# A routing stage with its sums on VectorE from SBUF, transposes in four PSUM banks and ranks behind the second gate

## What is computed

```python
x = x + _L0_gnn_ref(_layernorm(x, axis=-1), src, dst, edge_weight)   # 25000 edges, sums in float16
# feed-forward: h = layernorm(x)
logits = h @ gate_w + gate_b                    # 50000 x 8
idx = argmax(softmax(logits)); prb = its probability
pos = (cumsum(one_hot(idx)) * one_hot(idx)).sum(-1) - 1     # the token's rank with its expert
kept = pos < C                                  # C = ceil(1.25 * 50000 / 8)
y = (relu(buf @ w1 + b1) @ w2 + b2)[idx, pos] * (prb * kept)
x = x + y
```

## Time and profile before

| | before |
|---|---|
| median of three runs | 3391.64 us |
| profiled execution | 3385.78 us |
| its span | 3384.2 us |
| PE busy | 2856.8 us (84%) |
| DVE busy | 2205.4 us (65%) |
| ACT busy | 1627.8 us (48%) |
| POOL busy | 1881.3 us (56%) |
| mean granted clock of PE | 0.886 |

### The profile page before, as it was taken

One profiled execution on the slowest core, in us unless ns is written; L12 is line 12 of the kernel. 1 busy time (PEld: TensorE's weight loads), 2 busy tenths in 40 slices (PEclk: granted clock), 3 DMA queues, 4 the chain that ended last, 5 costly groups with the idle time before them and its releaser, 6 DMA issues.

```text
span 3384.2 us, 63776 instructions
## 1 busy us (share of the span) xinstructions
PE 2856.8 (84%) x20366; PEld 2577.6 (76%) x20367; DVE 2205.4 (65%) x5550; ACT 1627.8 (48%) x2915; POOL 1881.3 (56%) x1680
## 2 busy tenths in 40 slices
PE   5733323289899976999999999999999999999998
PEld 4733223278788866989889898989899889898987
DVE  7934343377766644677766767777767676767766
ACT  3412121156655644555554555555555555555554
POOL 7788888756766765436354334536343454335333
PEclk8766666678867868999999999999999999999999
DMA  9644443386766623112112111212111121111111
GB/s 375 193 77 71 69 88 58 52 321 230 245 207 221 234 75 101 45 39 74 39 50 69 44 45 45 67 36 71 45 50 44 42 69 48 44 43 47 41 46 45
DMA packets 182245, 322.06 MB, mean 95 GB/s; under 512 B 97649, under 2 KB 124348, under 8 KB 166256
## 3 DMA queue, kind: packets, MB, share of 16 engines
q0 software_dynamic: 89696, 146.98, 16.7%
q1 hardware_dynamic: 92288, 172.66, 15.0%
q10 hardware_dynamic: 144, 1.05, 0.1%
HBM read 186.52 MB, written 138.79 MB: 96 GB/s over the span
## 4 chain that ended last, share of the span: by engine, by line
PE 57%; DVE 3%; issue 1%; DVEq 0%; POOL 0%; DMA 0%; SPq 0%; ACT 0%; POOLq 0%
PE u_Y L1353 29%; PE u_H L1339 26%; PE u_T L1321 2%; DVE y L1283 1%; DVE y L1278 1%; DVE yo L1297 1%; DVE yo L1294 0%; DVE low L1288 0%; DVE yo L1292 0%; DVE hlo L1265 0%; POOL u_x L1141 0%; DVEq L1264 0%; DMA u_x<-out_x,u_rec 0%; DVE u_token L1291 0%; DMA u_rec<-slots 0%
## 5 line engine op out<-in xcount | busy, mean ns | idle before, releaser
L1166 POOL DMA_INDIRECT out_x<-yo,u_token x348 | 435.8, 1252 | 761.0 <-DVE yo L1299 664.2
L1353 PE MATMUL u_Y<-whi,hhi 128*128 128x256 f32 x2784 | 788.2, 283 | 22.2 <-DVE hlo L1265 22.2
L1216 ACT ACTIVATE hm<-u_H,b1e 128x512 f32<-128x512 f32 (+1 forms) x736 | 489.0, 664 | 644.5 <-PE u_H L1339 618.9
L1353 PE MATMUL u_Y<-wlo,hhi 128*128 128x256 f32 x2784 | 779.7, 280 | 0.0
L1353 PE MATMUL u_Y<-whi,hlo 128*128 128x256 f32 x2784 | 779.4, 280 | 0.0
L1141 POOL DMA_INDIRECT u_x<-out_x,u_rec x380 | 396.5, 1043 | 363.4 <-issue 330.0
L1339 PE MATMUL u_H<-xhi,whi 128*128 128x512 f32 (+1 forms) x1472 | 571.5, 388 | 10.1 <-issue 10.1
L1339 PE MATMUL u_H<-xlo,whi 128*128 128x512 f32 (+1 forms) x1472 | 564.8, 384 | 0.0
L1339 PE MATMUL u_H<-xhi,wlo 128*128 128x512 f32 (+1 forms) x1472 | 564.5, 384 | 0.0
L1353 PEld LDWEIGHTS u_Y<-whi,hhi 128*128 128x128 f32 x2784 | 526.1, 189 | 25.3 <-DVE hlo L1265 25.3
L1353 PEld LDWEIGHTS u_Y<-wlo,hhi 128*128 128x128 f32 x2784 | 526.1, 189 | 0.0
(11 more groups left out here) (154 smaller groups left out, 4710.5 us busy)
## 6 DMA issues: line engine op xcount, KB each, us to landing
x<-in_x SPq DMA_DIRECT2D x49, 1024.0 KB
out_x<-x SPq DMA_DIRECT2D x49, 1024.0 KB, 5.0
agg<-zeros SPq DMA_DIRECT2D x25, 1024.0 KB
at<-agg SPq DMA_DIRECT2D x49, 512.0 KB, 5.8
raw<-in_L_ffn_w POOLq DMA_DIRECT2D x14, 1024.0 KB
src_row<-in_src SPq DMA_DIRECT2D x25, 512.0 KB, 4.8
slots<-rec,slot_i POOLq DMA_INDIRECT x392
u_x<-out_x,u_rec POOLq DMA_INDIRECT x380
```

What stands on the lines that cost most here:

```text
L1166: pool.indirect_dma_start(out=out[:, :], out_offset=bass.IndirectOffsetOnAxis(ap=token[:, s:s + 1], axis=0), in_=yo[:, s, :], in_offset=No ...
L1216: act.activation(hm[:, f, cols], ps_H[:, f % 2, cols], ACT.Relu, bias=b1e[:, f:f + 1])\
L1353: last = pe.matmul(ps_Y[:, s, 0:D], a[:, f, rows], w2_at(w, buf, f), start=(f == 0 and j == 0), stop=(f == KF - 1 and j == 2))
```

## The change

`add` reads `at` from SBUF instead of its copy in PSUM, and waits for the load itself. `aggregate`, `ident16`, `ps_A` and `agg_up` are gone; SP's `load` waits for `x1_ready` four steps back. The four PSUM banks go to `ps_T`, one for each quarter, `ps_L` gets two banks, one for every other step, and the unread products get a bank of their own. `gated` is raised by every gate, and a copy waits for the same quarter's gate of the step before. `fill` issues three products of 512 columns in place of four of 384. The order of a step on PE becomes turn 0, turn 1, turn 2, fill, gate 0, turn 3, gate 1, rank of the step before, gate 2, fill, gate 3.

```diff
-    ident16 = sb("ident16", [P, P], F16)
...
-    ps_A = ctx.enter_context(nc.psum_tensor("ps_A", [P, G, D], F32))
-    ps_T = ctx.enter_context(nc.psum_tensor("ps_T", [P, 2, 4, P], F32))
-    ps_L = ctx.enter_context(nc.psum_tensor("ps_L", [P, 512], F32))
+    ps_T = ctx.enter_context(nc.psum_tensor("ps_T", [P, 4, 4, P], F32))
+    ps_L = ctx.enter_context(nc.psum_tensor("ps_L", [P, 2, 512], F32))
     ps_R = ctx.enter_context(nc.psum_tensor("ps_R", [P, 512], F32))
-    logits = ps_L[:, 0:G * E].rearrange("p (g e) -> p g e", g=G)
+    unread = ctx.enter_context(nc.psum_tensor("unread", [P, 4, P], F32))
+    logits = ps_L[:, :, 0:G * E].rearrange("p b (g e) -> p b g e", g=G)
     ranks = ps_R[:, 0:(G + 1) * E].rearrange("p (g e) -> p g e", g=G + 1)
-    unread = ps_L[:, P:4 * P].rearrange("p (n c) -> p n c", n=3)
-    FILL = 4
+    FILL = 3
...
                 if not (isinstance(i, int) and s < AGGS):
-                    sp.wait_ge(agg_up, s + 1 - AGGS)
+                    sp.wait_ge(x1_ready, s + 1 - AGGS)
                     sp.nop(nofuse=True)
...
-                    if k == 0 and not (isinstance(i, int) and s < 1):
-                        act.wait_ge(gated, s)
+                    if not (isinstance(i, int) and s < 1):
+                        act.wait_ge(gated, BANKS * (s - 1) + k + 1)
                     act.wait_ge(turned, BANKS * s + k + 1)
                     part = slice(k * PER_BANK, (k + 1) * PER_BANK)
-                    act.activation(hT[:, part, :], ps_T[:, k % 2], ACT.Copy).then_inc(hT_ready, 1)
+                    act.activation(hT[:, part, :], ps_T[:, k], ACT.Copy).then_inc(hT_ready, 1)
...
+                normalise(2)
                 copy(0)
-                normalise(2)
+                normalise(3)
                 copy(1)
-                normalise(3)
                 copy(2)
                 copy(3)
...
-            def aggregate(i, r):
-                s = RING * i + r
-                pe.wait_ge(agg_loaded[r % AGGS], 16 * ((RING // AGGS) * i + r // AGGS + 1))
-
-                if not (isinstance(i, int) and s == 0):
-                    pe.wait_ge(x1_ready, s)
-                for g in range(G):
-                    last = pe.matmul(ps_A[:, g, :], ident16[:], at[:, r % AGGS, g, :], start=True, stop=True)
-                last.then_inc(agg_up, 1)
...
                 if k == 0:
-                    if not (isinstance(i, int) and s < 1):
-                        pe.wait_ge(hot_ready, s)
-                    pe.matmul(logits, ident[:], gb[:].unsqueeze(1).broadcast_to([P, G, E]),
+                    if not (isinstance(i, int) and s < 2):
+                        pe.wait_ge(hot_ready, s - 1)
+                    pe.matmul(logits[:, q], ident[:], gb[:].unsqueeze(1).broadcast_to([P, G, E]),
...
-                if k == BANKS - 1:
-                    last.then_inc(gated, 1)
+                last.then_inc(gated, 1)
...
                 for _ in range(FILL):
-                    pe.matmul(unread, ones[:], before[:].unsqueeze(1).broadcast_to([P, 3, P]),
-                              start=False, stop=True, skip_group_check=True)
+                    pe.matmul(unread[:], ones[:], before[:].unsqueeze(1).broadcast_to([P, 4, P]),
+                              start=True, stop=True)
...
-                if not (isinstance(i, int) and s < 1 and k < 2):
-                    pe.wait_ge(hT_ready, BANKS * s + k - 1)
+                if not (isinstance(i, int) and s < 1):
+                    pe.wait_ge(hT_ready, BANKS * (s - 1) + k + 1)
...
                 turn(i, r, 0)
                 turn(i, r, 1)
-                if isinstance(i, int) and s == 0:
-                    aggregate(0, 2)
-                else:
+                turn(i, r, 2)
+                fill()
+                gate(i, r, 0)
+                turn(i, r, 3)
+                gate(i, r, 1)
+                if not (isinstance(i, int) and s == 0):
                     rank(*before_of(i, r, 1))
-                    fill()
-                gate(i, r, 0)
-                turn(i, r, 2)
-                gate(i, r, 1)
-                turn(i, r, 3)
-                if not (isinstance(i, int) and s == 0):
-                    fill()
                 gate(i, r, 2)
-                if not (isinstance(i, int) and s > LAST - 3):
-                    aggregate(*((i, r + 3) if r + 3 < RING else (i + 1, r + 3 - RING)))
+                fill()
                 gate(i, r, 3)
...
-                v.wait_ge(agg_up, s + 1)
+                v.wait_ge(agg_loaded[r % AGGS], 16 * ((RING // AGGS) * i + r // AGGS + 1))
                 v.wait_ge(x_loaded[r], 16 * (i + 1))
-                v.tensor_tensor(x1[:, r], ps_A[:], x1[:, r], ALU.add).then_inc(x1_ready, 1)
+                v.tensor_tensor(x1[:, r], at[:, r % AGGS], x1[:, r], ALU.add).then_inc(x1_ready, 1)
...
-                v.wait_ge(gated, s + 1)
-                v.tensor_reduce(top[:], logits, AX.X, ALU.max).then_inc(chosen, n.inc())
+                v.wait_ge(gated, BANKS * (s + 1))
+                v.tensor_reduce(top[:], logits[:, q], AX.X, ALU.max).then_inc(chosen, n.inc())
```

More of the change, by code:

```diff
@@ L489, in route_tokens @@
     agg_loaded = [sem(f"agg_loaded{r}") for r in range(AGGS)]
-    agg_up = sem("agg_up")
     x1_ready = sem("x1_ready")
@@ L510, in route_tokens @@
     BANKS = G * KD * P // 512
+    assert BANKS == 4
     PER_BANK = G * KD // BANKS
@@ L712, in gate @@
                     for kd in range(KD):
-                        last = pe.matmul(logits[:, g, :], hT[:, g * KD + kd, :], gw[:, kd, :],
+                        last = pe.matmul(logits[:, q, g, :], hT[:, g * KD + kd, :], gw[:, kd, :],
                                          start=False, stop=(kd == KD - 1), skip_group_check=True)
-                if k == BANKS - 1:
-                    last.then_inc(gated, 1)
+                last.then_inc(gated, 1)
             def fill():
                 for _ in range(FILL):
-                    pe.matmul(unread, ones[:], before[:].unsqueeze(1).broadcast_to([P, 3, P]),
-                              start=False, stop=True, skip_group_check=True)
+                    pe.matmul(unread[:], ones[:], before[:].unsqueeze(1).broadcast_to([P, 4, P]),
+                              start=True, stop=True)
             def turn(i, r, k):
@@ L727, in turn @@
                 pe.wait_ge(h_ready, BANKS * s + k + 1)
-                if not (isinstance(i, int) and s < 1 and k < 2):
-                    pe.wait_ge(hT_ready, BANKS * s + k - 1)
+                if not (isinstance(i, int) and s < 1):
+                    pe.wait_ge(hT_ready, BANKS * (s - 1) + k + 1)
                 for n in range(PER_BANK):
                     g, kd = divmod(k * PER_BANK + n, KD)
-                    last = pe.transpose(ps_T[:, k % 2, n, :], h[:, q, g, kd * P:(kd + 1) * P], ident[:])
+                    last = pe.transpose(ps_T[:, k, n, :], h[:, q, g, kd * P:(kd + 1) * P], ident[:])
                 last.then_inc(turned, 1)
@@ L739, in body @@
                 turn(i, r, 1)
-                if isinstance(i, int) and s == 0:
-                    aggregate(0, 2)
-                else:
-                    rank(*before_of(i, r, 1))
-                    fill()
-                gate(i, r, 0)
-                turn(i, r, 2)
-                gate(i, r, 1)
-                turn(i, r, 3)
-                if not (isinstance(i, int) and s == 0):
-                    fill()
+                turn(i, r, 2)
[4 more added lines that the diff above has]
+                if not (isinstance(i, int) and s == 0):
+                    rank(*before_of(i, r, 1))
                 gate(i, r, 2)
-                if not (isinstance(i, int) and s > LAST - 3):
-                    aggregate(*((i, r + 3) if r + 3 < RING else (i + 1, r + 3 - RING)))
+                fill()
                 gate(i, r, 3)
             pe.wait_ge(vector_set, 1)
-            aggregate(0, 0)
             pe.wait_ge(consts, 48)
-            pe.transpose(ps_L[:, 0:B1], b1r[:], ident[0:B1, 0:B1]).then_inc(b1_turned, 1)
-            aggregate(0, 1)
+            pe.transpose(ps_L[:, 0, 0:B1], b1r[:], ident[0:B1, 0:B1]).then_inc(b1_turned, 1)
             pe.wait_ge(b1_ready, 1)
@@ L774, in _ @@
         def _(v):
-            v.tensor_copy(ident16[:], ident[:])
             v.memset(stride[:], float(STEP))
@@ L828, in choice @@
                 last_step = isinstance(i, int) and s == LAST
-                v.wait_ge(gated, s + 1)
-                v.tensor_reduce(top[:], logits, AX.X, ALU.max).then_inc(chosen, n.inc())
+                v.wait_ge(gated, BANKS * (s + 1))
+                v.tensor_reduce(top[:], logits[:, q], AX.X, ALU.max).then_inc(chosen, n.inc())
                 v.wait_ge(chosen, n.now())
                 less = rec[:, r, :, LOGIT:LOGIT + E]
-                v.tensor_tensor(less, logits, top[:].unsqueeze(2).broadcast_to([P, G, E]), ALU.subtract)\
+                v.tensor_tensor(less, logits[:, q], top[:].unsqueeze(2).broadcast_to([P, G, E]), ALU.subtract)\
```

(2 more changed lines are left out.)

## The result

The changed kernel took 3435.5 us (median of six runs, 3417.0 to 3443.3), the kernel before 3390.7 us beside it (3371.4 to 3397.2): a ratio of 1.0135, interval 1.0095 to 1.0175. It is slower, by about 45 us. The profiled execution took 3436.45 us, which is 50.7 us more than that of before.

What follows compares the result with a forecast made beforehand. GpSimd's scatters were to bound the routing stage: 502.7 us scatters + 70.4 held + 3 later start + 14 idle gave 590 against 559.2, +31 us; forecast 3422 us, range 3376 to 3470.

Steps and rivals of the forecast that it cites:

- the rival with the low clock: Routing stage: more than half of TensorE's steps run at 13.5 us; 3452 us; decides above 11.8 us; chance 0.22.
- The signs that the forecast named: Routing stage: held scatters of 1.9 to 3.2 us, waits for slot_i well under 57 us, clock 0.6 to 0.75.
- The hold of a scatter: Routing stage: each sum from SBUF holds one scatter until 0.87 us after it; 46 sums, 70.4 us (41 to 100).
- GpSimd sets the pace: Routing stage: with held scatters GpSimd needs 11.8 us a step, 10.26 before, and so sets the stage's time.
- TensorE's clock: Routing stage: TensorE's mean step is 11 to 11.5 us at a somewhat lower clock, 13.5 us if all low.
- The identity products: Routing stage: removing eight per step takes 0.87 us off TensorE's step at the upper clock level, 1.66 at the lower.
- Idle that is left: Routing stage: GpSimd keeps a quarter of its 57 us without work, 14 us.
- The start: Routing stage: the first scatter starts 3 us later, about 6 by later ranks less some 3 by two aggregates fewer.
- The sum at 2.28 us: Routing stage: VectorE's sum of 2048 columns takes 2.28 us with both inputs in SBUF, the same rate as from PSUM.
- Ranks cost nothing beyond the pace: Routing stage: ranks behind the second gate make slots late, but no later than TensorE; no cost beyond the pace counted.

Runs made afterwards that it cites:

- early ranks: The changed kernel with the ranks moved back to where they were before, behind the second transposes: 3424.2 us, ratio 1.0135.

## Why the prediction came out as it did

The direction and the range were right, 3422 forecast and 3435.5 measured, about halfway to the 3452 of the rival with the low clock. The signs that the forecast named came too: 46 held scatters of 1.89 to 3.07 us, waits of 28 us in the stretch, a clock of 0.61. But only half of the stage went as the forecast had it. Point by point:

- **The hold of a scatter.** Right in mechanism and size. 74.4 us against 70.4, a mean scatter of 1.168 us against 1.17, the held ones ending 0.85 us behind the sum. The clause of the Trainium skill (SBUF — State Buffer, Who interferes with whom) by which `tensor_tensor` does not stall GpSimd's DMAs does not hold here.
- **GpSimd sets the pace.** This is the step that failed in part. It holds in the kernel with more unread products and in the one with the sum from SBUF alone, where its waits are under 6 and 8 us, and in the second half of the changed kernel's stretch. Over the whole stretch the slots came every (1294.6 - 713.6)/48 = 12.1 us on average, above the 11.8 from which I had the low clock's rival decide.
- **How much is the holds', how much the late slots'.** That depends on which is taken away first, since one hides the other. Without the holds, my estimate for the changed kernel is an end at 1309.0 us: the slots of the last step but two are ready at 1277.66 (the row below), then come 0.87 us to the first scatter, two steps of 10.26 and 9.96 for the last. The holds' own share of the 51 us is then 5.7. Put into the kernel before, they cost 22.6 us of stretch, 18 in the medians. The late slots are worth some 20 us by the kernel with more unread products; what it keeps of the loss, 23 us, is near what the sum from SBUF costs alone.

```profile
1277.49 0.17 DVE L857 SCALAR_TENSOR_TENSOR slot_i<-where,full 128x8 int32<-128x8 f32 x1
```

- **TensorE's clock.** I took a pace of 11 to 11.5 us at a somewhat lower clock; it was 12.1 at 0.61. The steps at the lower clock were predicted at 13.5 us and are 13.55. That the clock costs is shown by the run with more unread products: 0.80, and 20 us won. The changed kernel's own six runs say the same: 3439.5 and 3443.3 us at a mean clock of 0.855 and 0.854 over the whole kernel, 3417.0 and 3420.9 at 0.863 and 0.865.
- **The identity products.** Counted as 0.87 to 1.66 us of work taken off the path. That work is gone, and a step at the lower clock is 1.6 us shorter for it (13.55 against 15.15). But TensorE stayed at 1.2 GHz for the eight steps from 735 to 843 us, and each of them is longer than the 11.4 us that a step took on average before. Whether the removal, the new order or the place of the ranks brought the clock down is not separated on the first chip, and stays open.
- **Idle that is left.** 14 us forecast, 600.2 - 502.7 - 74.4 = 23 measured, all in the first half.
- **The start.** 3 us forecast, 10.2 measured. The ranks' part is seen: from choice to slots 8.1 us in step 0, and 3.7 before; early ranks gave 5.5 us back. I missed two things. TensorE was at the lower clock through the whole opening (0.50 against 0.62 before in 684 to 706 us). And two of the first sums took 3.10 and 3.42 us, beside eight `tensor_tensor` operations of GpSimd's own; these eight took 13.92 us where they had taken 9.85 beside the sums from PSUM. The hold works both ways.
- **The sum at 2.28 us.** Right: its median is 2.284 us.
- **Ranks cost nothing beyond the pace.** VectorE stood 85 us for them. Early ranks cut that wait to 5 us, and its wait for the gate grew from 100 to 123, so a part of it only moved. Whether the rest cost time is open: the medians can't be told apart, and the one profiled run had slots every 11.3 us in place of 12.1.

The 20 us by which the profiled execution exceeds the forecast sum are thus 7 at the start, 9 of idle and 4 of holds. The median came nearer than the reasons deserved: the forecast gave the whole loss to the holds, and by the runs about 20 of the 45 us go with TensorE's clock, which the sum had at nothing beyond its 14 us of idle. That the total still fell into the range is partly luck.

## What to carry to other kernels

When an engine issues indirect DMAs back to back, count what every long VectorE operation with two SBUF inputs adds to it: here one held DMA each, from the operation's start or later to 0.85 us behind its end. Don't take work off TensorE for its time alone: read the granted clock of the stage before and after, and price the step at both levels. With a queue between two stages of work, look for the last moment at which the second one waited: before it the first sets the pace, behind it the second. And if two causes hide each other, give what each costs alone, since their shares don't add up.

## What was not expected of the hardware

- Sums of 256 columns took 0.418 us each, and eight in a row 2.77 us from the first one's start to the last one's end, less than eight times 0.418, so they overlap; one sum of 2048 columns takes 2.28.
- A sum of VectorE from SBUF was itself held by GpSimd's `tensor_tensor`: 3.42 us in place of 2.28. In eight pieces it took 10.96.
- TensorE with less work stayed at its lower level for 108 us, in equal steps of 13.5 us, while with 2048 more unread columns a step the stretch had a mean clock of 0.80.
- The same kernel took 3392 us on one chip and 3584 to 3612 on others. The sum from SBUF cost 0.6% on the first; together with the removal of the products, which never ran on the first, it gained 1.7% on both of the others.
